# Four input homes for the feed-forwards, the variance of the weighted attention on VectorE, the causal mask in quarters

## Chip, cores and metric

One NeuronCore of a Trainium2 chip. The metric is device time in microseconds of one execution; a kernel's number is the median of its runs.

## The reference, cut to what matters

A batch of 64 sequences of 128 tokens and 128 features goes through four layers, each against a context of 77 tokens with 128 features. All tensors are float32.

```
x: [64, 128, 128]   context: [64, 77, 128]   16 heads
L0: att = softmax(causal(QK^T / sqrt(8))) V;  h = LayerNorm(att + x);  x = gelu(h W1 + b1) W2 + b2 + h
L1: att = softmax(mask(QK^T / sqrt(8) * weights)) V;  x = LayerNorm(x + att Wo + bo)      (LN_EPS 1e-5)
L2: att = softmax(mask(QK^T) / sqrt(128)) V;  h = LayerNorm(att Wo + bo + x);  x = LayerNorm(relu(h W1 + b1) W2 + b2 + h)
L3: n = RMSNorm(x);  x = x + segmented causal attention(n, 16 heads of 64, rotary) Wout;
    h = RMSNorm(x) W1 + b1;  a, g = split(h);  x = x + (silu(g) * a) W2 + b2
```

The causal mask of L0 forbids key k for query i when k > i: of 77 keys and 128 queries, queries 77 and later see all keys.

## The kernel before, in words

The layers are cut into seven stages that run one after another over all 64 batches: A0 and F0 (attention and feed-forward of L0), A1 (L1), A2 and F2 (L2), A3 and F3 (L3). Each stage reads its input from device memory and writes its output there. The program is written out by hand for each engine: for each stage an engine has a function `step(b, has)` that lists what it does in one step, for several batches at different depths of the pipeline, and `drive` runs the steps, the middle ones in a hardware loop of four. The engines meet only by counting semaphores, and every engine works its list in order. So the order in a step function is the order of execution, and a wait holds up all that stands behind it on that engine.

**Attention stages A0, A1, A2** (64 batches each). SyncE issues every DMA. TensorE (`cross_tensor`) computes, per batch, the keys, values and queries, the scores of 16 heads into four PSUM banks (four matmuls of 32 rows, one per group of four heads, line 668), transposes the probabilities in two halves of eight heads (line 686), and forms the attended values (line 703). In A0 the causal mask enters as a matmul of a bfloat16 identity with the tile `causal` (128 x 308: one 128 x 77 mask repeated for four heads), accumulated in PSUM before the scores: for banks 0 and 1 in `mask_early` at the end of the step before (line 650), for banks 2 and 3 at the head of `scores` (line 665). In A2 a bias per key is added behind the scores by four matmuls of one row (line 674). ScalarE takes the exponentials (line 769) and copies the transposed probabilities out of PSUM (line 774).

In A1 the scores are multiplied on VectorE by weights (line 886, two halves), masked by a `scalar_tensor_tensor` of the uint8 mask and the scores, both in SBUF (line 891, two halves), and reduced to a maximum (line 899); GpSimd subtracts the maximum (`shift`, line 1012, two halves: the second half of batch b first in its step, the first half of batch b + 1 later). The layer norm of batch b - 3 rides in the same steps: VectorE's `aggregate` (line 953) gives mean and variance; GpSimd adds the epsilon (line 1024), takes the power -1/2 (line 1026), and forms -mean x rstd (line 1035, a 128 x 1 result); ScalarE's `centre` computes z = t x rstd + that shift (line 820); GpSimd multiplies by gamma (line 1040) and adds beta (line 1043). GpSimd's step in A1, in order:

```
shift(b, 1); rstd(b - 3) [epsilon, power]; residual(b - 1); scale_mean(b - 3); shift(b + 1, 0); affine(b - 3) [gamma, beta]
```

and VectorE's: two `weigh`, `mask` of half 0, `invert`, `peak_masked` of half 0, `normalise`, `keep_v`, `sums`, `mask` of half 1, `statistics`, `peak_masked` of half 1, `aggregate`. In A0 and A2 GpSimd itself centres (line 1030).

**Feed-forward stages F0, F2, F3** (32 groups of two batches). TensorE (`ff_tensor`), per step: the hidden layer of group g (line 1154), the transposes of group g + 1 (line 1142), the down projection of group g - 1 (line 1168). The input of a group lies in `fx_s`, one tile per parity (two homes), loaded by `ff_sync` (line 1110) two groups ahead. A load waits until the home's last group has been transposed (in F3: normalised) and until GpSimd has added the bias to it (`residual`, line 1302). That residual of group g + 1 stands behind GpSimd's other work of the step; in F3 that is `rstd(g + 2)` (line 1312), which waits for VectorE's `squares(g + 2)` (line 1219), which waits for the load of group g + 2. VectorE in F3, per step: `norm(g + 1)` (line 1226), three `gate` (line 1234), `squares(g + 2)`, `total(g - 1)` (line 1247). The first two loads of a feed-forward stage are issued during the last steps of the stage before (`HEADS`, line 1935); the third waits in SyncE's list behind the last stores of that stage.

Of the kernel before, what the change touches and what calls it, by code (L numbers as in the profile page):

```python
# [138 lines left out]
def build_layers(nc, a, out):  # L139
# [3 lines left out]
    with ExitStack() as ctx:  # L143
# [31 lines left out]
        causal = sb("causal", [T, QC], BF16)  # L175
# [117 lines left out]
        shift_s = slots("mean_shift", [T, 1])  # L293
# [5 lines left out]
        fx_s = slots("fx", [T, GB, D])  # L299
# [44 lines left out]
        causal32, tri32 = wvo[:, 0:QC], wvo[:, 512:512 + HC * SEG]  # L344
        causal_loads = [(causal32, a["c_causal"])]
# [75 lines left out]
        mean_scaled = event("mean_scaled", ["A1"])  # L421
# [191 lines left out]
        def cross_tensor(pe, ph):  # L613
# [29 lines left out]
            def mask_early(b, values):  # L643
                if b.first:
                    pe.wait_ge(masks_made, 3)
                pe.wait_ge(k_kept.sem(b), k_kept.count(ph, b))
                if values:
                    pe.wait_ge(v_kept.sem(values), v_kept.count(ph, values))
                for c in range(2):
                    nc.tensor.matmul(bank[c][:, 0:QC], identb[:], causal[:], start=True, stop=False)  # L650

            def scores(b):
# [10 lines left out]
                if ph == "A0":  # L663
                    for c in range(2, NQ):
                        nc.tensor.matmul(bank[c][:, 0:QC], identb[:], causal[:], start=True, stop=False)
                for c in range(NQ):
                    rows = slice(32 * c, 32 * c + 32)
                    mm = nc.tensor.matmul(bank[c][:, 0:QC], qT_s[b.par][rows, :], kblk_s[b.par][rows, :],  # L668
                                          start=(ph != "A0"), stop=(ph != "A2"))
# [61 lines left out]
            def step(b, has):  # L731
# [28 lines left out]
                if has(2) and ph == "A0":  # L760
                    mask_early(b + 2, b + 1 if has(1) else None)
            drive(pe, NB, step, reach=REACH)

        def cross_scalar(act, ph):
# [52 lines left out]
            def centre(b):  # L817
                act.wait_ge(mean_scaled.sem(b), mean_scaled.count(ph, b))
                wait_earlier(act, zg_made, ph, b, 2)
                nc.scalar.activation(z_s[b.par][:], t_s[b.par][:], ACT.Identity, bias=shift_s[b.par][:, 0:1], scale=rstd_s[b.par][:, 0:1])\  # L820
                    .then_inc(z_made.sem(b), 1)

# [12 lines left out]
            def step(b, has):  # L835
# [17 lines left out]
                if has(-3) and weighted:  # L853
                    centre(b + -3)
# [8 lines left out]
        def cross_vector(dve, ph):  # L863
# [90 lines left out]

            def step_weighted(b, has):
                if has(1):
                    weigh(b + 1, 0)
                    weigh(b + 1, 1)
                    mask(b + 1, 0)
# [41 lines left out]
        def cross_gpsimd(pool, ph):  # L1001
# [20 lines left out]
            def rstd(b):  # L1022
                pool.wait_ge(mv_made.sem(b), mv_made.count(ph, b))
                nc.gpsimd.tensor_tensor(var_s[b.par][:], mv_s[b.par][:, 1:2], ln_eps[:, 0:1], ALU.add).then_inc(var_made.sem(b), 1)  # L1024
                pool.wait_ge(var_made.sem(b), var_made.count(ph, b))
# [6 lines left out]

            def scale_mean(b):

                nc.gpsimd.tensor_scalar(shift_s[b.par][:], mv_s[b.par][:, 0:1], rstd_s[b.par][:, 0:1], -1.0, ALU.mult, ALU.mult)\  # L1035
                    .then_inc(mean_scaled.sem(b), 1)
# [8 lines left out]
            def step(b, has):  # L1045
                weighted = ph == "A1"
                if weighted:
                    if has(0):
                        shift(b, 1)
                    if has(-3):  # L1050
                        rstd(b + -3)
                        wait_earlier(pool, z_made, ph, b + -3, 2)
                    if has(-1):
                        residual(b + -1)
                    if has(-3):
                        scale_mean(b + -3)
# [36 lines left out]
        def ff_sync(sp, ph):  # L1093
# [3 lines left out]
            def step(g, has):  # L1097
                if has(2):
                    n = g + 2

                    if (n + -2).exists:
                        sp.wait_ge(taken.sem(n + -2), taken.count(ph, n + -2))
                    if (n + -2).exists:
                        sp.wait_ge(fxb_made[ph].sem(n + -2), fxb_made[ph].count(ph, n + -2))
# [1038 lines left out]
```

## Time and profile before

| | |
|---|---|
| median of 3 runs | 2474.96 us (2472.53 to 2475.68) |
| the profiled execution, its time | 2471.87 us |
| its span, first to last instruction | 2470.1 us |
| mean granted TensorE clock | 0.985 of full |
| busy: TensorE, VectorE, ScalarE, GpSimd | 93%, 76%, 61%, 63% of the span |
| chain that ended last | TensorE 68%, GpSimd 16%, issue 6%, ScalarE 3%, VectorE 3%, DMA 2% |
| A0, F0 | about 0 to 383 us, 383 to 512 us |
| A1 (with the memory set-up before it), A2 | 512 to 961 us, 961 to 1312 us |
| F2, A3, F3 | 1312 to 1447 us, 1447 to 2320 us, 2320 to 2470 us |

"Busy" is the share of the span in which an engine has an instruction running. The chain is followed back from the last instruction: at each step to whatever released it. A line number names the line of the kernel that issued an instruction. In the views, PE is TensorE's matmul and PEld its weight load, DVE is VectorE, ACT ScalarE, POOL GpSimd, SPq SyncE's issue of a DMA. `sb_region` is one large tile in which the attention's working tiles are carved.

### The profile page before, as it was taken

How to read it: one execution, taken by the hardware profiler on the slowest of the kernel's cores; microseconds unless marked ns; L12 is line 12 of the kernel's file. 1: busy time of each engine (PE TensorE's matmuls, PEld its weight loads, DVE VectorE, ACT ScalarE, POOL GpSimd, SP SyncE). 2: the span in 40 equal slices, each digit the busy share in tenths (PEclk: the TensorE clock that was granted, in tenths of full speed). 3: DMA queues.
4: the chain of work that ended last, by engine and by line, in shares of the span. 5: the costliest groups of instructions: out<-in, count | busy, mean ns of one | idle time of the engine just before them, and what ended most of it. 6: DMA issues, size and time to landing. Idle time of an engine off the chain costs nothing.

```text
span 2470.1 us, 83369 instructions
## 1 busy us (share of the span) xinstructions
PE 2308.8 (93%) x26926; PEld 1812.7 (73%) x26926; DVE 1888.0 (76%) x4003; ACT 1498.6 (61%) x3408; POOL 1559.2 (63%) x2438
## 2 busy tenths in 40 slices
PE   7999998988888887999998989999999999999899
PEld 5777777976666665777777867777777777777687
DVE  5777772139999996777775678888888888888566
ACT  5777775549988996888885524444444444444433
POOL 2666663118999995666666766666666666666332
PEclk9999999979999998999999999999999999999999
DMA  4111111235555552222221223334333333333211
GB/s 128 43 43 42 42 42 55 72 96 164 162 162 159 165 162 49 52 50 51 50 50 52 67 76 95 93 96 97 96 94 95 94 94 95 93 94 93 54 58 53
DMA packets 443043, 211.78 MB, mean 86 GB/s; under 512 B 206400, under 2 KB 433856, under 8 KB 442816
## 3 DMA queue, kind: packets, MB, share of 16 engines
q1 hardware_dynamic: 442944, 210.51, 32.7%
q8 instruction: 56, 0.92, 0.2%
q14 instruction: 43, 0.35, 0.1%
HBM read 113.36 MB, written 29.88 MB: 58 GB/s over the span
## 4 chain that ended last, share of the span: by engine, by line
PE 68%; POOL 16%; issue 6%; ACT 3%; DVE 3%; DMA 2%; SPq 1%; POOLq 1%; DVEq 0%; ACTq 0%
PE bank L686 10%; PE bank L1463 9%; PE bank L1423 9%; POOL sb_region L1012 5%; PE bank L703 5%; PE bank L1491 5%; PE bank L1154 4%; PE bank L668 4%; PE bank L1168 4%; PE bank L1473 3%; PE bank L1449 3%; ACT sb_pT L774 3%; POOL sb_mean_shift L1035 2%; POOL sb_var L1024 2%; PE bank L1499 2%
## 5 line engine op out<-in xcount | busy, mean ns | idle before, releaser
L686 PE MATMUL bank<-sb_ident,sb_region 128*77 128x128 f32 x3072 | 413.1, 278 | 57.4 <-ACT sb_pT L774 54.0
L774 ACT ACTIVATE sb_pT<-bank 77x1024 f32<-77x1024 f32 x384 | 391.6, 1020 | 81.4 <-PE bank L686 80.4
L686 PEld LDWEIGHTS bank<-sb_ident,sb_region 128*77 128x77 f32 x3072 | 348.3, 151 | 112.1 <-issue 108.2
L1553 ACT ACTIVATE sb_l<-sb_l 128x640 f32<-128x640 f32 x128 | 94.5, 738 | 384.6 <-DVE sb_l L1601 384.6
L873 DVE TENSOR_REDUCE sb_max<-bank 128x8 f32<-128x616 f32 x256 | 203.1, 793 | 151.1 <-PE bank L668 80.3
L769 ACT ACTIVATE sb_region<-sb_region 128x616 f32<-128x616 f32 x384 | 276.9, 722 | 25.0 <-POOL sb_region L1012 24.9
L1680 POOL TENSOR_TENSOR sb_pn<-sb_l,sb_r_all 128x512 f32<-128x512 f32 x128 | 134.7, 1052 | 232.1 <-DVE sb_r_all L1611 224.2
L1423 PE MATMUL bank<-sb_region,sb_wqkv 128*128 128x128 f32 x2048 | 253.7, 278 | 5.8 <-DVE sb_region L1589 5.0
L1463 PE MATMUL bank<-sb_wvo,sb_region 128*64 128x512 f32 x1024 | 248.2, 606 | 0.0
L1423 PEld LDWEIGHTS bank<-sb_region,sb_wqkv 128*128 128x128 f32 x2048 | 241.9, 194 | 8.3 <-DVE sb_region L1589 5.6
L703 PEld LDWEIGHTS bank<-sb_pT,sb_v 77*32 77x32 f32 x6144 | 152.3, 110 | 93.4 <-issue 73.4
L703 PE MATMUL bank<-sb_pT,sb_v 77*32 77x128 f32 x6144 | 216.2, 277 | 3.8 <-ACT sb_pT L774 3.6
L878 DVE TENSOR_TENSOR sb_region<-bank,sb_max 128x616 f32<-128x616 f32 x256 | 204.6, 799 | 11.7
L1671 POOL TENSOR_TENSOR sb_region<-sb_region 128x512 f32<-128x512 f32 x128 | 162.6, 1270 | 72.6 <-PE bank L1449 64.5
L668 PE MATMUL bank<-sb_region,sb_qT 32*128 32x308 f32 x1536 | 158.2, 481 | 33.8 <-ACT sb_region L789 20.4
L1012 POOL TENSOR_TENSOR sb_region<-sb_region,sb_max 128x616 f32<-128x616 f32 x128 | 158.8, 1241 | 37.5 <-DVE sb_max L899 37.5
L1491 PEld LDWEIGHTS bank<-sb_region,sb_pT 128*64 128x64 f32 x2048 | 121.7, 137 | 77.4 <-issue 67.5
L1024 POOL TENSOR_TENSOR sb_var<-sb_mv,sb_ln_eps 128x1 f32<-128x1 f32 x192 | 68.0, 354 | 174.8 <-DVE sb_mv L953 174.8
L1203 ACT ACTIVATE sb_fh<-bank,sb_L_xattn_ffb 128x256 f32<-128x256 f32 x256 | 109.0, 472 | 113.7 <-PE bank L1154 113.7
L1537 ACT ACTIVATE sb_region<-bank 128x512 f32<-128x512 f32 x256 | 151.3, 593 | 41.5 <-PE bank L1463 32.0
L1589 DVE TENSOR_TENSOR sb_region<-bank,sb_sinT 128x512 f32<-128x512 f32 x256 | 174.0, 680 | 0.0
L1589 DVE TENSOR_TENSOR sb_region<-bank,sb_cosT 128x512 f32<-128x512 f32 x256 | 172.5, 674 | 1.6 <-PE bank L1423 1.5
(184 smaller groups left out, 5629.1 us busy)
## 6 DMA issues: line engine op xcount, KB each, us to landing
sb_region<-in_side SPq DMA_DIRECT2D x64, 616.0 KB, 3.8
sb_pT<-sb_region SPq DMA_DIRECT2D x512, 64.0 KB, 2.0
sb_kF<-sb_region SPq DMA_DIRECT2D x512, 64.0 KB, 2.2
scratch_after_A<-sb_y SPq DMA_DIRECT2D x256, 64.0 KB, 1.7
sb_fx<-scratch_after_A SPq DMA_DIRECT2D x96, 128.0 KB, 2.1
sb_mask<-in_mask SPq DMA_DIRECT2D x64, 154.0 KB, 2.3
sb_x<-scratch_after_F SPq DMA_DIRECT2D x128, 64.0 KB, 1.9
sb_ctx<-in_ctxT SPq DMA_DIRECT2D x192, 38.5 KB, 1.8
```

Source lines behind the costliest of these rows:

```text
L668: mm = nc.tensor.matmul(bank[c][:, 0:QC], qT_s[b.par][rows, :], kblk_s[b.par][rows, :], start=(ph != "A0"), stop=(ph != "A2"))
L686: mm = nc.tensor.transpose(two[0:C, h * T:(h + 1) * T], p_s[b.par][:, head * C:(head + 1) * C], ident[:])
L703: mm = nc.tensor.matmul(att_bank[32 * i:32 * i + 32, k * T:(k + 1) * T], v_s[b.par][:, first:first + 32], pT_s[k][:, h * T:(h + 1) * T], s ...
L769: nc.scalar.activation(half(p_s[b.par], k), half(p_s[b.par], k), ACT.Exp, scale=SCALE[ph]).then_inc(exp_made.sem(b), 1)
L774: nc.scalar.activation(pT_s[k][:], two[0:C, :], ACT.Copy).then_inc(pT_kept.sem(b), 1)
L873: nc.vector.tensor_reduce(dst, by_bank_and_head(scores_half(k)), AX.X, ALU.max).then_inc(max_made.sem(b), 1)
L878: nc.vector.tensor_tensor(by_bank_and_head(by_bank(half(p_s[b.par], k))), by_bank_and_head(scores_half(k)), spread_max(k), ALU.subtract).t ...
L1012: nc.gpsimd.tensor_tensor(by_head(half(p_s[b.par], k)), by_head(half(p_s[b.par], k)), spread(max_s[:, 8 * k:8 * k + 8], C), ALU.subtract)\
L1423: mm = nc.tensor.matmul(rope_bank[eo][:, n * T:(n + 1) * T], wqkv[:, col:col + 128], xnT_s[b.lap], start=True, stop=True)
L1463: mm = nc.tensor.matmul(vo_banks[g][r * SEG:(r + 1) * SEG, :], xnT_s[b.lap][:, g * SEG:(g + 1) * SEG], wvo[:, (2 * h + r) * HC * D:(2 * h ...
L1491: nc.tensor.matmul(out3_bank[g * SEG:(g + 1) * SEG, 0:D], pT_s3[h][:, c * T + g * SEG:c * T + (g + 1) * SEG], vo_s[h][:, (g * HC + c) * D: ...
L1589: ins = nc.vector.tensor_tensor(part[what][eo].rearrange("p (n t) -> p n t", t=T), src, table[:].unsqueeze(1).to_broadcast([128, BLOCKS, T ...
```

## The change

1. **A0's mask in quarters.** `mask_early` and the mask matmuls ahead of the scores go. The scores now open each bank's accumulation, and behind them come eight matmuls of 64 rows and 64 columns: per bank one for queries 0 to 63 and one for queries 64 to 127, from 64 x 64 pieces of the identity, placed so that four neighbouring ones use the four quarters of the array. The tile `causal` shrinks to 128 x 154 and is loaded by two DMAs in place of one; the wait for it becomes a wait for two.
2. **A1's layer norm.** GpSimd's addition of epsilon goes to VectorE (`variance`, between the second `weigh` and the first `mask`). GpSimd's `scale_mean` and ScalarE's `centre` go; GpSimd now centres itself, by the instruction that it uses in A0 and A2, at the place where `scale_mean` stood.
3. **Feed-forwards.** `fx_s` has four homes; a group is loaded four ahead, into the home of group n - 4, and waits besides for the load of group n - 2. The first four loads of a stage are issued in the last steps of the stage before.

```diff
-        causal = sb("causal", [T, QC], BF16)
+        causal = sb("causal", [T, 2 * C], BF16)
...
-        fx_s = slots("fx", [T, GB, D])
+        fx_s = slots("fx", [T, GB, D], n=LAPS)
...
-        causal32, tri32 = wvo[:, 0:QC], wvo[:, 512:512 + HC * SEG]
-        causal_loads = [(causal32, a["c_causal"])]
+        causal32, tri32 = wvo[:, 0:2 * C], wvo[:, 512:512 + HC * SEG]
+        causal_loads = []
+        for r in range(2):
+            both = a["c_causal"].rearrange("(g i) (h k) -> i g h k", g=2, k=C)
+            causal_loads.append((causal32[r * KH:(r + 1) * KH, :].rearrange("p (g k) -> p g k", k=C), both[:, :, 0, :]))
...
-            def mask_early(b, values):
-                if b.first:
+            def scores(b):
+                if ph == "A0" and b.first:
                     pe.wait_ge(masks_made, 3)
-                pe.wait_ge(k_kept.sem(b), k_kept.count(ph, b))
-                if values:
-                    pe.wait_ge(v_kept.sem(values), v_kept.count(ph, values))
-                for c in range(2):
-                    nc.tensor.matmul(bank[c][:, 0:QC], identb[:], causal[:], start=True, stop=False)
-
-            def scores(b):
...
-                if ph == "A0":
-                    for c in range(2, NQ):
-                        nc.tensor.matmul(bank[c][:, 0:QC], identb[:], causal[:], start=True, stop=False)
                 for c in range(NQ):
                     rows = slice(32 * c, 32 * c + 32)
                     mm = nc.tensor.matmul(bank[c][:, 0:QC], qT_s[b.par][rows, :], kblk_s[b.par][rows, :],
-                                          start=(ph != "A0"), stop=(ph != "A2"))
+                                          start=True, stop=(ph == "A1"), skip_group_check=(ph == "A0"))
+                if ph == "A0":
+                    for c in range(NQ):
+                        for g in range(2):
+                            r = (g + c) % 2
+                            rows = slice(r * KH, (r + 1) * KH)
+                            later = causal[rows, g * C:(g + 1) * C].unsqueeze(1).to_broadcast([KH, QH, C])
+                            mm = nc.tensor.matmul(bank[c][g * KH:(g + 1) * KH, 0:QC], identb[rows, r * KH:(r + 1) * KH], later,
+                                                  start=False, stop=True, skip_group_check=True)
...
-                if has(2) and ph == "A0":
-                    mask_early(b + 2, b + 1 if has(1) else None)
...
-            def centre(b):
-                act.wait_ge(mean_scaled.sem(b), mean_scaled.count(ph, b))
-                wait_earlier(act, zg_made, ph, b, 2)
-                nc.scalar.activation(z_s[b.par][:], t_s[b.par][:], ACT.Identity, bias=shift_s[b.par][:, 0:1], scale=rstd_s[b.par][:, 0:1])\
-                    .then_inc(z_made.sem(b), 1)
...
-                if has(-3) and weighted:
-                    centre(b + -3)
...
+            def variance(b):
+                dve.wait_ge(mv_made.sem(b), mv_made.count(ph, b))
+                nc.vector.tensor_scalar(var_s[b.par][:], mv_s[b.par][:, 1:2], LN_EPS, None, ALU.add).then_inc(var_made.sem(b), 1)
...
                 if has(1):
                     weigh(b + 1, 0)
                     weigh(b + 1, 1)
+                if has(-3):
+                    variance(b + -3)
+                if has(1):
                     mask(b + 1, 0)
...
                     if has(-3):
-                        rstd(b + -3)
-                        wait_earlier(pool, z_made, ph, b + -3, 2)
+                        root(b + -3)
                     if has(-1):
                         residual(b + -1)
                     if has(-3):
-                        scale_mean(b + -3)
+                        centre(b + -3)
...
-                if has(2):
-                    n = g + 2
+                if has(LAPS):
+                    n = g + LAPS
+
+                    if (n + -LAPS).exists:
+                        sp.wait_ge(taken.sem(n + -LAPS), taken.count(ph, n + -LAPS))
+                        sp.wait_ge(fxb_made[ph].sem(n + -LAPS), fxb_made[ph].count(ph, n + -LAPS))
 
                     if (n + -2).exists:
-                        sp.wait_ge(taken.sem(n + -2), taken.count(ph, n + -2))
-                    if (n + -2).exists:
-                        sp.wait_ge(fxb_made[ph].sem(n + -2), fxb_made[ph].count(ph, n + -2))
+                        sp.wait_ge(fx_loaded.sem(n + -2), fx_loaded.count(ph, n + -2))
...
-                    sp.dma_start(fx_s[n.par][:], pair_of(source[ph], n)).then_inc(fx_loaded.sem(n), 16)
+                    sp.dma_start(fx_s[n.lap][:], pair_of(source[ph], n)).then_inc(fx_loaded.sem(n), 16)
...
-            HEADS = {ph: () if ph == "A3" else (-2, -1) if ph in FFS else (-4, -3) for ph in order}
+            HEADS = {ph: () if ph == "A3" else (-4, -3, -2, -1) if ph in FFS else (-4, -3) for ph in order}
...
-            dve.wait_ge(causal_loaded, 1 * 16)
+            dve.wait_ge(causal_loaded, 2 * 16)
```

`LAPS` is 4. All readers of `fx_s` index it by `lap` instead of `par`. `root` is the second half of the old `rstd`: the wait for `var_made`, the power, and the wait for its own result.

## Rows read from the trace of the kernel before

**Rows 1.** Timeline, TensorE, one batch of A0: start, us, engine, line, out<-in, xcount, idle before.
```profile
201.29 1.07 PE L686 MATMUL bank<-sb_ident,sb_region 128*77 128x128 f32 x8 [0.25 <-ACT sb_pT L774]
...
202.81 0.80 PE L668 MATMUL bank<-sb_region,sb_qT 32*128 32x308 f32 x8
203.54 0.43 PE L703 MATMUL bank<-sb_pT,sb_v 77*32 77x128 f32 x8
```

**Rows 2.** Timeline, TensorE, the same steps in A2, which has no causal mask.
```profile
1024.42 1.07 PE L686 MATMUL bank<-sb_ident,sb_region 128*77 128x128 f32 x8
1025.48 0.80 PE L668 MATMUL bank<-sb_region,sb_qT 32*128 32x308 f32 x8
```

**Rows 3.** Timeline, TensorE, A3: four 64x64 tiles and what starts behind them.
```profile
1605.38 0.30 PE L1441 MATMUL bank<-sb_tri,sb_identb 64*64 64x256 bf16 x4
1605.52 0.73 PE L1449 MATMUL bank<-sb_kF,sb_pT 64*64 64x81 f32 x32
```

**Rows 4.** Window of A1: us, busy us (x instructions) of PE, PEld, DVE, ACT, POOL.
```profile
563.00:938.00 375.00, 314.47 (x4030) 241.62 (x4030) 354.52 (x715) 337.59 (x769) 348.42 (x476) 1.00 0.54 160
```

**Rows 5.** Timeline, VectorE and GpSimd, one batch of A1.
```profile
750.16 1.21 POOL L1012 TENSOR_TENSOR sb_region<-sb_region,sb_max 128x616 f32<-128x616 f32 x1
...
750.92 1.12 DVE L891 SCALAR_TENSOR_TENSOR sb_region<-sb_mask,sb_region 128x616 f32<-128x616 uint8 x1
...
751.34 0.75 POOL L1024 TENSOR_TENSOR sb_var<-sb_mv,sb_ln_eps 128x1 f32<-128x1 f32 x1
...
752.16 0.55 POOL L1026 TENSOR_TENSOR sb_rstd<-sb_var,sb_minus_half 128x1 f32<-128x1 f32 x1
...
753.37 1.01 POOL L1035 TENSOR_SCALAR sb_mean_shift<-sb_mv,sb_rstd 128x1 f32<-128x1 f32 x1
753.46 0.79 DVE L891 SCALAR_TENSOR_TENSOR sb_region<-sb_mask,sb_region 128x616 f32<-128x616 uint8 x1
```

**Rows 6.** Timeline, A1 near its start: a root issued just after a mask.
```profile
561.92 0.79 DVE L891 SCALAR_TENSOR_TENSOR sb_region<-sb_mask,sb_region 128x616 f32<-128x616 uint8 x1
...
562.04 1.08 POOL L1026 TENSOR_TENSOR sb_rstd<-sb_var,sb_minus_half 128x1 f32<-128x1 f32 x1
```

**Rows 7.** Groups by line: the centring as GpSimd does it in A0 and A2.
```profile
L1030 POOL TENSOR_SCALAR sb_z<-sb_t,sb_mv,sb_rstd 128x128 f32<-128x128 f32 x128 | 102.1, 797 | 0.4
```

**Rows 8.** One line: VectorE's tensor_scalar in F2, ns min/median/max.
```profile
L1273 DVE TENSOR_SCALAR sb_fc<-sb_ft,sb_fmv x64: 286/519/795, 1325.0 to 1445.0; 128x128 f32<-128x128 f32 x64
```

**Rows 9.** Timeline, head of F0: residual, third load, TensorE.
```profile
390.28 1.40 POOL L1302 TENSOR_TENSOR sb_fxb<-sb_fx,sb_L_xattn_ffb 128x256 f32<-128x256 f32 x2
391.07 1.07 SPq L1110 DMA_DIRECT2D sb_fx<-scratch_after_A  x2
...
393.31 0.62 PE L1142 MATMUL bank<-sb_ident,sb_fx 128*128 128x128 f32 x2 [4.26 <-DMA sb_fx<-scratch_after_A]
...
396.97 1.89 PE L1154 MATMUL bank<-sb_fxT,sb_L_xattn_ffw 128*128 128x256 f32 x8
```

**Rows 10.** Waits of TensorE in F2, from 1318 to 1440 us: total, times, longest.
```profile
PE bank L1142 <- DMA sb_fx<-scratch_after_A: 1.8, 2, 1.4
```

**Rows 11.** Timeline, TensorE in F3: four starts of down projections.
```profile
2327.89 1.50 PE L1168 MATMUL bank<-sb_w2g,sb_fh 128*128 128x128 f32 x12
...
2450.74 1.50 PE L1168 MATMUL bank<-sb_w2g,sb_fh 128*128 128x128 f32 x12
...
2454.89 1.50 PE L1168 MATMUL bank<-sb_w2g,sb_fh 128*128 128x128 f32 x12
...
2463.38 2.84 PE L1168 MATMUL bank<-sb_w2g,sb_fh 128*128 128x128 f32 x24
```

**Rows 12.** Timeline, F3: from one load of the input to the next residual.
```profile
2375.84 0.38 SPq L1110 DMA_DIRECT2D sb_fx<-scratch_after_A  x1
...
2378.27 0.29 DVE L1219 CUSTOM_DVE_ANT_0 sb_fsq<-sb_fx 128x128 f32<-128x128 f32 x1 [0.75 <-DMA sb_fx<-scratch_after_A]
...
2379.62 0.72 POOL L1302 TENSOR_TENSOR sb_fxb<-sb_fx,sb_L_xattn_ff_b 128x256 f32<-128x256 f32 x1
```

More of the change, by code:

```diff
@@ L292, in build_layers @@
         rstd_s = slots("rstd", [T, 1])
-        shift_s = slots("mean_shift", [T, 1])
         z_s = slots("z", [T, D])
@@ L420, in build_layers @@
         rstd_made = event("rstd_made", CROSS)
-        mean_scaled = event("mean_scaled", ["A1"])
         z_made = event("z_made", CROSS)
@@ L1024, in rstd, with root @@
                 nc.gpsimd.tensor_tensor(var_s[b.par][:], mv_s[b.par][:, 1:2], ln_eps[:, 0:1], ALU.add).then_inc(var_made.sem(b), 1)
+                root(b)
+            def root(b):
                 pool.wait_ge(var_made.sem(b), var_made.count(ph, b))
@@ L1031, in centre @@
                                         ALU.subtract, ALU.mult).then_inc(z_made.sem(b), 1)
-            def scale_mean(b):
-                nc.gpsimd.tensor_scalar(shift_s[b.par][:], mv_s[b.par][:, 0:1], rstd_s[b.par][:, 0:1], -1.0, ALU.mult, ALU.mult)\
-                    .then_inc(mean_scaled.sem(b), 1)
             def affine(b):
@@ L1140, in transpose_x @@
                         pe.wait_ge(fx_loaded.sem(g), fx_loaded.count(ph, g))
-                        src = fx_s[g.par][:, k, :]
+                        src = fx_s[g.lap][:, k, :]
                     mm = nc.tensor.transpose(fx_bank[g.par][:, k * T:(k + 1) * T], src, ident[:])
@@ L1218, in squares @@
                 for k in range(GB):
-                    nc.vector.tensor_tensor_reduce(fsq_s[k][:], fx_s[g.par][:, k, :], fx_s[g.par][:, k, :], 1.0 / D, RMS_EPS, ALU.mult, ALU.add,
+                    nc.vector.tensor_tensor_reduce(fsq_s[k][:], fx_s[g.lap][:, k, :], fx_s[g.lap][:, k, :], 1.0 / D, RMS_EPS, ALU.mult, ALU.add,
                                                    fvar_s[g.par][:, k:k + 1]).then_inc(fstats_made.sem(g), 1)
@@ L1225, in norm @@
                     dve.wait_ge(fxT_made[ph].sem(g + -2), fxT_made[ph].count(ph, g + -2))
-                nc.vector.tensor_tensor(fz_s[g.par][:], fx_s[g.par][:], spread(frstd_s[g.par][:], D), ALU.mult).then_inc(fz_made[ph].sem(g), 1)
+                nc.vector.tensor_tensor(fz_s[g.par][:], fx_s[g.lap][:], spread(frstd_s[g.par][:], D), ALU.mult).then_inc(fz_made[ph].sem(g), 1)
             def gate(g):
@@ L1301, in residual @@
                     pool.wait_ge(ft_made.sem(g + -2), ft_made.count(ph, g + -2))
-                nc.gpsimd.tensor_tensor(fxb_s[g.par][:], fx_s[g.par][:], every(b2), ALU.add).then_inc(fxb_made[ph].sem(g), 1)
+                nc.gpsimd.tensor_tensor(fxb_s[g.par][:], fx_s[g.lap][:], every(b2), ALU.add).then_inc(fxb_made[ph].sem(g), 1)
             def rstd(g):
```

## Prediction

> **What bounds the kernel now.** I read the page first: TensorE is busy for 93% of the span and makes up 68% of the chain that ended last, GpSimd 16%. Such shares are an average over seven stages, so I cut the trace into windows by stage, followed the chain of waits in one steady batch of each stage that the change touches, and read the timeline where stages meet.
>
> In A0 the chain of a batch runs through TensorE and one ScalarE copy. From the transposes of half 1 to the scores it is 1.52 us (202.81 - 201.29), from the scores to the attended values 0.73 us, 2.25 us together [rows 1]; the mask matmuls lie inside, nothing covers them.
>
> In A1 a batch takes 6.3 us (375 us hold 476 GpSimd instructions, eight a batch) with VectorE busy 95%, GpSimd 93%, ScalarE 90% [rows 4]. GpSimd never rests, but part of its busy time is waiting: the mask of VectorE and GpSimd's instructions shut each other out. The mask was issued at 750.92 and ended at 752.04, 0.67 us after GpSimd's shift ended at 751.37; the epsilon sum, one element a row, took 0.75 us, until that mask was done; the shift of the mean, also one element, took 1.01 us, until the next mask ended at 754.25 [rows 5].
>
> F0 and F2 are bound by TensorE except at their heads, where the third load is late. F3 is bound by a loop: a load is issued at 2375.84, the squares start at 2378.27, the residual ends at 2380.34, and only that lets the next load go, 4.5 us later and more [rows 12]. TensorE needs 4.15 us a group where nothing holds it (2450.74 to 2454.89) and gets one in 4.52 us on average (2327.89 to 2463.38, thirty intervals) [rows 11].
>
> **F3.** The load four ahead is freed by the same residual, but is needed two groups later, so the 2.4 us from issue to squares leave the loop. The squares then follow the gates, the root is done while TensorE runs its down projection, and the next bound is TensorE at 4.15 us. Full gain 30 x 0.37 = 11 us. VectorE's normalisation may still collide with GpSimd's residual and hold a gate, so I take **10 us**, range 6 to 11.5. The added wait for load n - 2 is met two groups before; behind it on SyncE stand the output stores, which nobody waits for until the group after next.
>
> **Head of F0.** Today the third load is issued at 391.07, after the residual of group 0 has started behind the tail of A0; TensorE idles 4.26 us until 393.31 and reaches the next hidden layer at 396.97 [rows 9]. With four loads in place it goes on at 389.05 with two transposes and a down projection: twelve such matmuls show 1.50 us [rows 11], sixteen and the transposes about 2.15 us, so the hidden layer starts at 391.2. Gain 5.8 us; I take **6**, range 5 to 6.5. It holds more than the idle time because the matmuls behind the gap ran slowly (3.66 us from 393.31 to 396.97 for the same work). **Head of F2:** the same wait is 1.8 us [rows 10]; **1.5 us**. The first four loads cost SyncE two more issues during A0, A2 and A3, about half a microsecond each [rows 9], where SyncE has slack.
>
> **A0.** The four mask matmuls leave the stretch before the scores. What remains there is what A2 shows: 1.06 us from the transposes to the scores (1025.48 - 1024.42) [rows 2], not 1.52 less four masks, because matmuls of another tile shape don't follow on at once. Behind the scores come two rounds of four quarters. In A3 four tiles of 64 x 64 with 256 columns let the next matmul start 0.14 us later [rows 3]; with 308 columns 0.17, two rounds 0.34 us. The quarters add one more change of tile shape; the one from the transposes to the scores costs about 0.2 us (1.06 us for eight transposes, which stream in some 0.86 if each takes an eighth of 1.07 less the last one's tail), and I take half of it for this one, between nothing and 0.2. New path 1.06 + 0.73 + 0.34 + 0.1 = 2.23, without that 0.1 and with perfect overlap of 0.26 it is 2.05. I take 2.19, a gain of 0.06 on 62 batches: **4 us**. Bounds: 0.20 gained a batch (12 us); two quarters at a time and not four, 0.16 lost (10 us). The page TensorEngine Tiling of the Trainium skill, section Tiling Modes, says that changing the tile shape drains the engine. The trace agrees, by the 0.2 us just named; by the rule the quarters cost a drain that masks of full height did not, and without it A0 would gain 0.10 more a batch. The wait for keys, formerly in part ahead of the early masks, is met: GpSimd's `block_keys` ends before the transposes do.
>
> **A1.** Count from the end M of mask 0, 752.04. Today the root starts at M + 0.12 and ends at M + 0.67, the mean's shift is released by mask 1 at about M + 2.3, and the second shift follows [rows 5]. Changed: the variance is on VectorE before mask 0, which anyway waits 0.45 us (750.92 to 751.37), so the root's input is ready when the shift ends, and the root is itself shut out by mask 0. How that ends the trace shows: a root issued 0.12 us after a mask ended 0.41 us behind it (563.12 against 562.71) [rows 6]. So root until M + 0.42; gap and residual take 0.66 today (752.71 to 753.37), less a little for a wait that goes: M + 1.0. Then the centring, 0.80 us [rows 7], until M + 1.8. Mask 1 is issued at M + 1.42 and finds the centring running: it ends 0.67 us after its release, M + 2.47. The second shift begins there and not at M + 2.3. Of the 0.17 lost I give back 0.1, as an instruction that is shut out has its start behind it (the root needed 0.41 after release, 0.55 when free [rows 5, 6]). The variance itself: nothing if it ends inside the wait of mask 0; if it is shut out too, at most 0.17, the 0.29 us of the fastest `tensor_scalar` [rows 8] less the 0.12 that the mask saves when shut out (0.67 for 0.79) [rows 5]. I take 0.05. Sum +0.12 us on 60 batches, **7 us lost**. ScalarE is relieved of a copy that was not on its path to the scores. Bounds: 0.25 gained (the root's 0.25 comes through) and 0.6 lost (rival 3). The page SBUF - State Buffer, section Who interferes with whom, says that `tensor_scalar` with both ends in SBUF can use two ports and then shuts GpSimd out, or is shut out, for a whole instruction. It speaks against both moved pieces. The same operation of VectorE in F2 takes 286 ns at best and 519 at the median [rows 8], so the trace agrees for 128 x 128; for one element a row nothing here shows it. By the rule A1 would lose 14 us and not 7.
>
> **Start.** One more DMA issue ahead of the first loads: **0.5 us** lost [rows 9].
>
> **Sum:** -10 - 6 - 1.5 - 4 + 7 + 0.5 = -14 us. Against the profiled execution, 2471.87, that is 2458; its time is 3.1 us below the median of 2474.96, against which the result is measured: **2461 us**.
>
> **Rivals.** (1) A1 gains: GpSimd holds the ports for only part of the centring, so mask 1 isn't delayed, and the earlier root counts, 0.2 gained a batch, 12 us. Sum -14 - 7 - 12 = -33: 2442, and 2434 with A0 at its good bound. For it: the centring computes long on few elements; against it: the mask waited for the full shift. Chance 0.2. (2) Only the feed-forwards pay: the quarters run two at a time, A0 loses 10 us. Sum 0, 2475. For it: nothing in A0 shows quarters; against it: A3 does. Chance 0.07. (3) Slower. In A1 GpSimd's work and VectorE's masks never overlap: root 0.42, gap and residual 0.66, centring 0.8, mask 0.79, shifts 2.42, gamma and beta about 0.9 (what today's 6.3 leaves), variance 0.17 and mask 0.71 add to 6.9 us against 6.3 now: +0.6 on 60 batches, 36 us lost and not 7. Sum +15: 2490. The place is mask 1 against the centring; it decides from +0.35 a batch, where the other gains (21 us) are eaten. For it: both engines are at 93% and above; against it: an instruction that is shut out keeps its start. Chance 0.08. (4) The change does not free F3: the normalisation collides every time and a group still takes 4.5 us. Sum -4, 2471. Chance 0.08. (5) The variance is shut out each time, and mask 0 with it, 0.12 + 0.12 a batch: A1 loses 14 us, sum -7: 2468. Chance 0.12. The forecast, between 2450 and 2466: 0.45.
>
> **How the numbers follow.** The measurement tells about 0.2%, 5 us, from no change. Faster by more: the forecast, rival 1, most of 5 and a part of 4, **0.77**. Within: rival 2, the rest, **0.14**. Slower: rival 3 and the far end of 2, **0.09**. The range of eight in ten takes the forecast, most of rival 1 and of 4 and 5: **2441 to 2475**.
>
> **What would show it.** F3: no wait of the squares for a DMA, starts of the down projections 4.15 to 4.25 us apart. F0: no idle time of 4 us near 389. A0: transposes to scores 1.06 us, scores to attended values 1.1 to 1.2 us. A1: mask 1 at 1.0 to 1.3 us instead of 0.79, mask 0 unchanged, the root at 1.1 us, a batch at 6.4 us. It is wrong if A1's batch is under 6.2 or over 6.6 us, or if scores to attended values in A0 is above 1.3 us.

## The result and the profile after

The new kernel took 2441.57 us (median of 4 runs, 2439.34 to 2442.62) against 2475.32 for the kernel before: 0.9865 of it, 95% interval 0.9847 to 0.9882. That is 33.8 us less, where 14 were forecast. It lies at the very edge of the range (2441 to 2475), and on rival 1 (2442).

The profiled executions differ by 29.3 us (2442.62 less 2471.87; spans 2440.8 and 2470.1). To see where these went I took the time line of TensorE and compared the start of the same matmul at the end of each stage. Differences to the kernel before in us, stretch by stage:

| stretch, to | forecast | new | homes alone | A1 alone | quarters alone |
|---|---|---|---|---|---|
| last scores of A0 | -3.5 | -4.0 | -1.8 | +0.7 | -3.9 |
| last hidden layer of F0 | -6 | -4.5 | -3.9 | 0.0 | +1.3 |
| last scores of A1 | +7 | **-8.8** | +1.8 | **-9.0** | -1.9 |
| last scores of A2 | 0 | -1.6 | -0.1 | -0.3 | +0.7 |
| last hidden layer of F2 | -1.5 | -5.2 | -6.1 | -1.5 | -0.2 |
| first masks of A3 | 0 | +2.5 | +3.4 | -0.1 | +0.9 |
| last masks of A3 | 0 | +0.7 | +3.5 | +4.6 | 0.0 |
| last hidden layer of F3 | -10 | -8.5 | -10.1 | +0.5 | +0.1 |

(The last three columns are told below.) Stretches that an edit does not touch differ by up to 2 us, A3 by up to 4.6, and one profiled execution may lie some us from its kernel's median; a single entry means no more than that. The entry that matters is A1's: it has the wrong sign.

The chain that ended last, by engine, in the new kernel's page: GpSimd's share fell from 16% to 12%.

```profile
PE 70%; POOL 12%; issue 8%; ACT 4%; DVE 2%; SPq 1%; DMA 1%; POOLq 0%; DVEq 0%; ACTq 0%
```

**A1**, window of the new kernel that answers to [rows 4] (us, then busy us and instructions of PE, PEld, DVE, ACT, POOL): GpSimd is as busy as before, with seven instructions a batch in place of eight, and VectorE has got idle time (355 to 341 us).

```profile
563.00:938.00 375.00, 311.65 (x4055) 247.00 (x4053) 340.89 (x776) 315.12 (x707) 351.79 (x430) 0.99 0.53 157
```

Time line of VectorE and GpSimd in one batch, which answers to [rows 5]:

```profile
737.72 1.22 POOL L1008 TENSOR_TENSOR sb_region<-sb_region,sb_max 128x616 f32<-128x616 f32 x1
...
738.63 0.14 DVE L946 TENSOR_SCALAR sb_var<-sb_mv 128x1 f32<-128x1 f32 x1
...
738.69 0.90 DVE L880 SCALAR_TENSOR_TENSOR sb_region<-sb_mask,sb_region 128x616 f32<-128x616 uint8 x1
...
738.89 1.12 POOL L1025 TENSOR_TENSOR sb_rstd<-sb_var,sb_minus_half 128x1 f32<-128x1 f32 x1
...
740.67 0.80 POOL L1029 TENSOR_SCALAR sb_z<-sb_t,sb_mv,sb_rstd 128x128 f32<-128x128 f32 x1
...
741.02 0.79 DVE L880 SCALAR_TENSOR_TENSOR sb_region<-sb_mask,sb_region 128x616 f32<-128x616 uint8 x1
...
741.44 1.44 POOL L1008 TENSOR_TENSOR sb_region<-sb_region,sb_max 128x616 f32<-128x616 f32 x1
```

Mask 0 ends at M = 739.59 (738.69 + 0.90). The root ends at 740.01, M + 0.42, as forecast; the centring begins at 740.67, M + 1.1, and ends at M + 1.9, each 0.1 us later than forecast. Mask 1 is issued at 741.02, M + 1.43, as forecast, with the centring running. The forecast let it wait until the centring had ended. It did not wait: it took 0.79 us, and the centring beside it 0.80. What is shut out is the shift behind them, which ends at 742.88, M + 3.3. Before, it ended at M + 3.5 (754.34 + 1.21 less 752.04), in the time line of [rows 5]:

```profile
754.34 1.21 POOL L1012 TENSOR_TENSOR sb_region<-sb_region,sb_max 128x616 f32<-128x616 f32 x1
```

The next mask 0 then finds less of the shift of half 1 in its way: between 590 and 900 us it takes 1.00 us on average, where it took 1.22 before. The forecast had it unchanged. That is 0.22 us a batch, less the 0.06 by which the added sum delays it; a batch takes 6.16 us in place of 6.32 (mean distance of the scores, 600 to 880 us).

One line each, over the whole run: the centring (min/median/max in ns), and the added sum on VectorE.

```profile
L1029 POOL TENSOR_SCALAR sb_z<-sb_t,sb_mv,sb_rstd x192: 792/797/906, 38.3 to 1297.2; 128x128 f32<-128x128 f32 x192
L946 DVE TENSOR_SCALAR sb_var<-sb_mv x64: 142/144/155, 554.5 to 932.6; 128x1 f32<-128x1 f32 x64
```

The first shows that the centring is not disturbed even once in A1: at most 906 ns in 192, and that also as the most in A0 and A2 before (907). The second takes 0.14 us at the median. In this batch mask 0 starts 0.02 us before the second `weigh` ends; in the batch of [rows 5] it started 0.08 us before. So the sum delays it by 0.06.

**A0**, time line of TensorE in one batch, which answers to [rows 1]:

```profile
199.98 1.07 PE L685 MATMUL bank<-sb_ident,sb_region 128*77 128x128 f32 x8 [0.25 <-ACT sb_pT L771]
...
201.04 0.80 PE L659 MATMUL bank<-sb_region,sb_qT 32*128 32x308 f32 x8
...
201.77 0.47 PE L667 MATMUL bank<-sb_causal,sb_identb 64*64 64x308 bf16 x8
...
202.17 1.08 PE L702 MATMUL bank<-sb_pT,sb_v 77*32 77x128 f32 x32
```

Transposes to scores 1.06 us, scores to quarters 0.73, quarters to attended values 0.40: 2.19 in all, each as forecast (0.34 + 0.1 for the quarters).

**Head of F0**, time line of TensorE, answering to [rows 9], and the granted clock (last columns: PEclk, DMA share, GB/s) in two windows of it:

```profile
380.32 3.49 PE L1149 MATMUL bank<-sb_fxT,sb_L_xattn_ffw 128*128 128x256 f32 x8 [0.53 <-ACT sb_fxT L1184]
...
384.65 1.99 PE L1149 MATMUL bank<-sb_fxT,sb_L_xattn_ffw 128*128 128x256 f32 x8 [0.62 <-ACT sb_fxT L1184]
...
388.49 1.89 PE L1149 MATMUL bank<-sb_fxT,sb_L_xattn_ffw 128*128 128x256 f32 x8
```

```profile
381.00:382.00 1.00, 1.00 (x4) 0.82 (x3) 0.93 (x6) 0.99 (x2) 0.82 (x2) 0.50 0.00 0
384.00:386.00 2.00, 1.38 (x7) 1.22 (x7) 0.00 (x0) 1.21 (x4) 1.73 (x4) 1.00 0.14 41
```

The first two hidden layers in the kernel before:

```profile
383.90 1.99 PE L1154 MATMUL bank<-sb_fxT,sb_L_xattn_ffw 128*128 128x256 f32 x8 [0.53 <-ACT sb_fxT L1189]
...
387.05 2.00 PE L1154 MATMUL bank<-sb_fxT,sb_L_xattn_ffw 128*128 128x256 f32 x8 [0.94 <-ACT sb_fxT L1189]
```

The wait of 4.26 us is gone. But the first hidden layer now takes 3.5 us where it took 2.0: the granted clock is at its lower level (0.50, 1.2 GHz) at 381 us, as the first hidden layer starts. Before, it fell at 393, behind the wait. From the second hidden layer to the third it is now 3.84 us (384.65 to 388.49) where it was 9.92 (387.05 to 396.97), 6.1 less; from the first to the second it is 4.33 where it was 3.15, 1.2 more.

**F3**, time line, answering to [rows 11, 12]: down projections, the addition of the bias on GpSimd and the normalisation on VectorE in two groups.

```profile
2383.64 1.50 PE L1163 MATMUL bank<-sb_w2g,sb_fh 128*128 128x128 f32 x12
...
2385.78 0.73 POOL L1297 TENSOR_TENSOR sb_fxb<-sb_fx,sb_L_xattn_ff_b 128x256 f32<-128x256 f32 x1 [0.24 <-DVE sb_ft L1242]
...
2385.89 0.90 DVE L1221 TENSOR_TENSOR sb_fz<-sb_fx,sb_frstd 128x256 f32<-128x256 f32 x1 [0.19 <-issue]
...
2388.00 1.50 PE L1163 MATMUL bank<-sb_w2g,sb_fh 128*128 128x128 f32 x12
...
2390.04 0.43 DVE L1221 TENSOR_TENSOR sb_fz<-sb_fx,sb_frstd 128x256 f32<-128x256 f32 x1
...
2390.14 0.91 POOL L1297 TENSOR_TENSOR sb_fxb<-sb_fx,sb_L_xattn_ff_b 128x256 f32<-128x256 f32 x1 [0.23 <-DVE sb_ft L1242]
...
2392.15 1.50 PE L1163 MATMUL bank<-sb_w2g,sb_fh 128*128 128x128 f32 x12
```

The squares no longer wait for a load. For most of the stage the groups take 4.15 and 4.36 us by turns. In the long ones the addition (2385.78) starts ahead of the normalisation (2385.89), which then takes 0.90 us in place of 0.43 and holds up a gate; in the short ones the normalisation is first and it is the addition that takes 0.91, which costs nothing: that group takes 4.15 us.

### The profile page after: what moved, and what is told of

It reads as the page before. It is cut to its first block, busy times and chain, and to the rows that moved or that the text cites. A ratio compares the mean times of both kernels' runs of the same rounds, so it can differ in the third digit from the quotient of the medians.

```text
span 2440.8 us, 83677 instructions
## 1 busy us (share of the span) xinstructions
PE 2287.5 (94%) x27182; PEld 1807.3 (74%) x27182; DVE 1872.0 (77%) x4067; ACT 1474.2 (60%) x3344; POOL 1562.2 (64%) x2374
## 4 chain that ended last, share of the span: by engine, by line
PE 70%; POOL 12%; issue 8%; ACT 4%; DVE 2%; SPq 1%; DMA 1%; POOLq 0%; DVEq 0%; ACTq 0%
PE bank L685 10%; PE bank L1458 9%; PE bank L1418 9%; PE bank L1149 6%; PE bank L702 5%; PE bank L1486 5%; PE bank L659 4%; PE bank L1163 4%; POOL sb_region L1008 4%; ACT sb_pT L771 3%; PE bank L1468 3%; PE bank L1444 3%; POOL sb_rstd L1025 2%; PE bank L1494 2%; POOL sb_z L1029 2%
## 5 line engine op out<-in xcount | busy, mean ns | idle before, releaser
L702 PE MATMUL bank<-sb_pT,sb_v 77*32 77x128 f32 x6144 | 208.8, 276 | 3.2 <-ACT sb_pT L771 3.2
L1666 POOL TENSOR_TENSOR sb_region<-sb_region 128x512 f32<-128x512 f32 x128 | 162.6, 1270 | 72.4 <-PE bank L1444 61.9
L1008 POOL TENSOR_TENSOR sb_region<-sb_region,sb_max 128x616 f32<-128x616 f32 x128 | 173.2, 1353 | 38.4 <-DVE sb_max L888 38.4
L1667 POOL TENSOR_TENSOR sb_region<-sb_region 128x512 f32<-128x512 f32 x128 | 165.9, 1296 | 0.0
```

Source lines behind the costliest of these rows:

```text
L702: mm = nc.tensor.matmul(att_bank[32 * i:32 * i + 32, k * T:(k + 1) * T], v_s[b.par][:, first:first + 32], pT_s[k][:, h * T:(h + 1) * T], s ...
L1008: nc.gpsimd.tensor_tensor(by_head(half(p_s[b.par], k)), by_head(half(p_s[b.par], k)), spread(max_s[:, 8 * k:8 * k + 8], C), ALU.subtract)\
```

## The experiments

**Each part alone.** Three kernels, each the kernel before with one part of the change: the homes; A1's layer norm; the quarters.

```diff
# homes
-        fx_s = slots("fx", [T, GB, D])
+        fx_s = slots("fx", [T, GB, D], n=LAPS)
...
# A1
-                        rstd(b + -3)
+                        root(b + -3)
...
-                        scale_mean(b + -3)
+                        centre(b + -3)
...
# quarters
-                    mask_early(b + 2, b + 1 if has(1) else None)
```

> The kernel before with the feed-forwards' part alone: four homes, loads four groups ahead. If the parts add up as the two traces put them: 8 us come from F3 (groups alternate between 4.15 and 4.36 us instead of 4.52 on average), 4 from F0, 3 from F2 with its hand-over to A3, together 15 us less, and A0 and A1 keep their batches of 5.56 and 6.3 us. If instead part of what the new kernel gains in the feed-forwards comes from the other two parts (an earlier end of A0 or A2), it is under 10 us.

> The kernel before with the part in A1 alone: variance on VectorE, centring on GpSimd, no sum and no shift of the mean there, no copy on ScalarE. Theory (the centring and the mask of VectorE run side by side): a batch takes 6.15 us, 9 us less in all. Forecast on record (the mask waits for the centring): 7 us more. If the gain in A1 is owed to the part in A0 or to the loads, no change.

> The kernel before with the quarter masks alone. As forecast: from the transposes to the scores 1.06 us, from the scores to the attended values 1.13, a batch of A0 5.50 us instead of 5.565, 4 us less in A0, and 0.5 us given back at the start: 3.5 us less. If the A0 gain of the new kernel is owed to something else, A0 keeps 5.565 us.

Measured: homes 2455.35 us, 0.9918 of the kernel before (0.9906 to 0.9931); A1 2464.26, 0.9961 (0.9949 to 0.9973); quarters 2470.51, 0.9988 (0.9980 to 0.9997). With 2473.54 before, that is 18, 9 and 3 us less, 30 together for the 34 of the whole: the parts add up within their intervals. The batches are as expected: in A0 5.50 us (median distance of the scores) with the quarters and 5.57 without, in A1 6.16 with A1's part and 6.33 without. The homes gave 3 us more than expected; with them alone only every fourth group of F3 is a long one, and F3 gains 10.1 us. So the gain of A1 belongs to A1's part.

**Which half of A1's part?** The centring on GpSimd, with the epsilon sum left there. Against the kernel with A1's part alone:

```diff
                if has(-3):
-                    variance(b + -3)
...
-                        root(b + -3)
+                        rstd(b + -3)
```

> The kernel before with the centring of A1 on GpSimd, the epsilon sum left there too. Theory (the centring runs beside the mask; the second shift starts when mask 1 ends, M + 2.2, whether the variance is early or late): sum until M + 0.12, root until M + 0.67, add until M + 1.33, centring M + 1.33 to 2.13, mask 1 M + 1.43 to 2.22, second shift until M + 3.3 as in the new kernel: 6.15 us a batch, 9 us less. Rival (the gain comes from the variance on VectorE): no change within 2 us, or slower, since GpSimd does 0.8 us of work that ScalarE did.

Measured: 2508.01 us, 1.0141 (1.0126 to 1.0157), 34 us **more**. Neither; the rival's "or slower" gave no such size, and its reason, the extra work, is in the new kernel too. Time line of a batch of the more frequent kind:

```profile
741.56 1.53 POOL L1027 TENSOR_SCALAR sb_z<-sb_t,sb_mv,sb_rstd 128x128 f32<-128x128 f32 x1
...
741.63 0.79 DVE L881 SCALAR_TENSOR_TENSOR sb_region<-sb_mask,sb_region 128x616 f32<-128x616 uint8 x1
```

Here the mask is issued 0.07 us behind the centring's start, and the centring takes 1.53 us: it ends 0.67 us after the mask does. The mask is not delayed. Between 590 and 900 us 29 of 44 batches look like this; in 13 others the centring meets no mask and takes 0.80 us. What differs here from the new kernel is the sum itself, 0.75 us on GpSimd, and with it the lead. That gave the next theory: what counts is by how much GpSimd's instruction starts ahead of the mask. The other half alone, the sum on VectorE with the shift of the mean and ScalarE's centring kept:

```diff
+                if has(-3):
+                    variance(b + -3)
...
                     if has(-3):
-                        rstd(b + -3)
+                        root(b + -3)
```

> The kernel before with only the variance moved: the epsilon sum of A1 on VectorE, the shift of the mean on GpSimd and the centring on ScalarE as before. Theory (what counts is the lead of GpSimd's instruction over mask 1: one whose start is 0.35 us ahead runs undisturbed, one 0.07 ahead is shut out): root until M + 0.42, add until M + 1.08, the shift of the mean issued 0.35 us ahead of mask 1 is over in 0.26 us, at M + 1.34. The second shift then starts ahead of mask 1 (M + 1.43) and the mask waits until it ends at M + 2.55: mask 1 takes 1.8 us instead of 0.79 and the batch grows by 0.3 to 0.8 us, 20 to 50 us more in all. Rival (the whole gain of A1 is the sum that left GpSimd): 9 us less.

Measured: 2467.77 us, 0.9980 (0.9970 to 0.9989), 4 us less, and 5.6 us less in the stretch of A1. The sign was missed. The shift of the mean behaved as foretold (0.27 us, undisturbed), but in 36 of 49 batches the mask then went ahead of the second shift, of 616 elements, though that had started before it:

```profile
751.27 0.27 POOL L1045 TENSOR_SCALAR sb_mean_shift<-sb_mv,sb_rstd 128x1 f32<-128x1 f32 x1
...
751.49 2.00 POOL L1019 TENSOR_TENSOR sb_region<-sb_region,sb_max 128x616 f32<-128x616 f32 x1
...
751.63 0.79 DVE L891 SCALAR_TENSOR_TENSOR sb_region<-sb_mask,sb_region 128x616 f32<-128x616 uint8 x1
```

Only in 13 batches did the mask wait for the shift, 1.58 us.

**The lead, changed by itself.** The new kernel, mask 1 one instruction earlier:

```diff
-                if has(-2):
-                    sums(b + -2)
                 if has(1):
                     mask(b + 1, 1)
                 if has(-2):
+                    sums(b + -2)
                     statistics(b + -2)
```

> The new kernel with mask 1 of A1 ahead of the sum with the residual on VectorE, so that the mask is issued 0.15 us behind the centring's start and not 0.35. Theory A (the centring needs the shared access for well under 0.15 us): centring and mask both keep 0.8 us, the second shift is shut out 0.2 us less, a batch takes 5.95 us instead of 6.15: 12 us less than the new kernel. Theory B (it needs it for 0.15 to 0.35 us): the centring is shut out and takes about 1.4 us, a batch 6.5: 20 us more than the new kernel.

Measured: 2471.03 us, 0.9994 (0.9984 to 1.0004): 29 us above the new kernel's 2441.57 (33 by the distance of each to the kernel before beside it), and the stretch of A1 is 28 us longer than there. A batch of A1 takes 6.67 us, 0.51 more, and nearly all of that stands at mask 0, which takes 1.48 us on average in place of 1.00, as the shifts behind the centring come later. This is theory B, dearer than its 20 us.

```profile
741.65 1.60 POOL L1028 TENSOR_SCALAR sb_z<-sb_t,sb_mv,sb_rstd 128x128 f32<-128x128 f32 x1
...
741.80 0.79 DVE L880 SCALAR_TENSOR_TENSOR sb_region<-sb_mask,sb_region 128x616 f32<-128x616 uint8 x1
```

All batches of A1 between 590 and 900 us in these kernels, by the time from the start of GpSimd's instruction to that of mask 1 (us, read off the time lines):

| kernel | GpSimd's instruction | lead | it took | mask 1 took |
|---|---|---|---|---|
| centring alone | centring | 0.06 to 0.08 (29 batches) | 1.52 to 1.54 | 0.79 |
| mask earlier | centring | 0.14 to 0.15 (35) | 1.59 to 1.61 | 0.79 |
| mask earlier | centring | 0.29 to 0.30 (11) | 1.58 to 1.59 | 0.79 |
| centring alone | centring | 0.33 to 0.34 (2) | 0.80 | 0.79 |
| centring alone | centring | no mask beside it (13) | 0.80 | - |
| new, A1 alone | centring | 0.34 to 0.50 (50 each) | 0.80 | 0.79 |
| before | shift of the mean | -0.01 to 0.25 (49) | 0.91 to 1.08 | 0.79 |
| variance alone | shift of the mean | 0.26 to 0.57 (49) | 0.27 | 0.79; 1.5 to 1.6 from 0.51 on |

The edge for the centring lies between 0.30 and 0.33 us. Below it the centring ends 0.5 to 0.7 us after the mask; above it the two run side by side, for 0.3 us or more. The one-element instruction takes 0.27 us undisturbed. With a lead of 0.25 or less it ends 0.05 to 0.13 us after the mask; with 0.26 or more it is over as the mask starts. So its rows don't show two instructions side by side; they show that it can be held by a mask that starts 0.25 us after it. In no batch did the centring delay the mask.

**The lead given back.** The kernel with the centring alone, with VectorE's statistics moved ahead of mask 1:

```diff
+                if has(-2):
+                    statistics(b + -2)
                 if has(1):
                     mask(b + 1, 1)
-                if has(-2):
-                    statistics(b + -2)
```

> The kernel with the centring on GpSimd and the epsilon sum left there, but the batch-norm statistics of VectorE ahead of mask 1 instead of behind it, so that the mask is issued 0.6 us behind the centring's start and not 0.07. Theory (a lead of 0.33 us or more leaves both undisturbed): the centring takes 0.80 us in place of 1.53, mask 1 keeps 0.79, and 10 to 25 us of the 34 that this kernel lost come back, though the mask itself is 0.5 us later. Rival (the loss is owed to the sum on GpSimd and mask 0 behind it, not to the lead): the centring may be short, but the time stays within 5 us of the kernel with the centring alone, or grows.

Measured: 2500.97 us, 1.0123 (1.0106 to 1.0140), 29 us above the kernel before beside it: 5 us of the 34 came back (4 in the stretch of A1), less than the theory said and within the rival's bound; the two intervals overlap.

```profile
741.91 0.80 POOL L1027 TENSOR_SCALAR sb_z<-sb_t,sb_mv,sb_rstd 128x128 f32<-128x128 f32 x1
...
742.68 1.21 POOL L1006 TENSOR_TENSOR sb_region<-sb_region,sb_max 128x616 f32<-128x616 f32 x1
...
742.78 1.76 DVE L881 SCALAR_TENSOR_TENSOR sb_region<-sb_mask,sb_region 128x616 f32<-128x616 uint8 x1
```

The centring takes 0.80 us in every batch, so the lead does what the theory says of it. But the lead became 0.87, not 0.6, and the mask, now 0.10 us behind the start of the second shift, waits for it: 1.76 us. There is an upper end to the useful lead as well: the mask has to come in before the shift. Nor is the rival's reason shown: mask 0 takes 0.79 us in every batch here, and 1.25 on average with the centring alone, against 1.22 before. So one loss took the place of another, and no run prices the short lead of the centring-alone kernel by itself; the earlier mask does that for the new kernel.

**A0: the place or the quarters?** The kernel before with its four masks of full height behind the scores:

```diff
+                if ph == "A0":
+                    for c in range(NQ):
+                        mm = nc.tensor.matmul(bank[c][:, 0:QC], identb[:], causal[:], start=False, stop=True)
```

> The kernel before with the four masks of full height behind the scores of A0. Theory (the place gives 0.46 us, 1.52 less 1.06; the masks cost 0.13 us each behind the scores, with no change of tile behind them): from the scores to the attended values 1.25 us, a batch 2.31 us on the path instead of 2.25, A0 4 us longer than before; the quarters then are worth 0.12 us a batch, 8 us. Rival (the place alone gives the gain): a batch of 5.50 us as with the quarters, 4 us less than before.

Measured: 2484.27 us, 1.0050 (1.0034 to 1.0066), 12 us more. Theory right in sign, low in size:

```profile
200.91 0.80 PE L658 MATMUL bank<-sb_region,sb_qT 32*128 32x308 f32 x8
...
201.65 0.70 PE L662 MATMUL bank<-sb_causal,sb_identb 128*128 128x308 bf16 x4
...
202.28 1.08 PE L696 MATMUL bank<-sb_pT,sb_v 77*32 77x128 f32 x32
```

Four masks take 0.63 us before the attended values start, not 0.52; a batch takes 5.75 us. The quarters do it in 0.40, so they are worth 0.23 us a batch, 14 us, and without them the new place would lose.

**F3: the collision.** The new kernel, the addition of F3 behind the normalisation, tried twice, the second time beside the new kernel again:

```diff
                if has(1):
+                    if has(2) and ph == "F3":
+                        pool.wait_ge(fz_made[ph].sem(g + 2), fz_made[ph].count(ph, g + 2))
                    residual(g + 1)
```

> The new kernel with GpSimd's addition of the bias in F3 behind the normalisation of VectorE, not beside it. Theory (every second group loses 0.2 us because the two shut each other out): all groups take 4.15 us, 3 us less than the new kernel. Rival (the 4.36 us come from TensorE or the gates): no change.

> The new kernel again, beside the next one on the same chip: 0.9865 of the kernel before.

> The new kernel with the addition of F3 behind the normalisation, a second time. Theory (3 us less in F3): 0.9853 of the kernel before, 3 us less than the new kernel beside it; rival: the same as the new kernel.

```profile
2380.60 0.42 DVE L1221 TENSOR_TENSOR sb_fz<-sb_fx,sb_frstd 128x256 f32<-128x256 f32 x1
...
2381.17 0.73 POOL L1297 TENSOR_TENSOR sb_fxb<-sb_fx,sb_L_xattn_ff_b 128x256 f32<-128x256 f32 x1 [0.73 <-DVE sb_fz L1221]
...
2382.78 1.50 PE L1163 MATMUL bank<-sb_w2g,sb_fh 128*128 128x128 f32 x12
...
2386.93 1.50 PE L1163 MATMUL bank<-sb_w2g,sb_fh 128*128 128x128 f32 x12
...
2391.08 1.50 PE L1163 MATMUL bank<-sb_w2g,sb_fh 128*128 128x128 f32 x12
```

Every group takes 4.15 us. From the first to the last hidden layer F3 is 11.4 us shorter than before in both profiles, against 8.5 and 7.1 in the new kernel's two: the 3 us of the theory or a little more. The whole: 2440.58 us (0.9866, 0.9843 to 0.9889) the first time, the same ratio as the new kernel's 0.9865; the second time 2436.63 (0.9857, 0.9840 to 0.9874) beside 2439.39 of the new kernel (0.9869, 0.9852 to 0.9885), 2.8 us lower with intervals that overlap. So the gain is shown in the stage, not in the whole.

## Why the prediction was wrong

- **A1, the failed step**: "Mask 1 is issued at M + 1.42 and finds the centring running: it ends 0.67 us after its release, M + 2.47." It ended at M + 2.2, undisturbed in each batch. The price 0.67 came from a mask behind a shift of 616 elements, which held the mask nearly to its end; it was applied to an instruction of 128 elements that held it in no batch. The gain then comes through at mask 0, 1.00 us in place of 1.22, which the forecast had unchanged; so the term of A1, +7, measured -8.8, and a batch of 6.16 us met the forecast's own sign of being wrong (under 6.2). I had written that mechanism down as rival 1, with nearly the right result for A1 (12 us gained, 9 measured), and gave it 0.2. The steps around it held: root at M + 0.42, centring at M + 1.1, mask issued at M + 1.43. My own sum thus had the centring 0.42 us ahead of the mask, and the 49 instructions of the kernel before, of one element and with leads of 0.25 at most, could not speak about that.
- **The Trainium skill**, page SBUF - State Buffer, section Who interferes with whom, calls the pair of ports that VectorE shares with GpSimd an exclusive lock, says of an instruction of VectorE with two SBUF inputs that it contends with GpSimd's reads, and that issue order decides who blocks. For the centring the runs disagree: issued first, it ran for 0.45 us of its 0.80 beside a mask of two SBUF inputs, and neither was longer; and with a lead of 0.30 us or less it was issued first and yet was the one held. Nor was the sum of one element on VectorE ever shut out (0.15 us at most, beside a shift of GpSimd), so rival 5, whose rule stands on the same page, did not happen.
- **Rival 3** (36 us lost in A1, mask 1 against the centring) had the place right: with the lead gone, the earlier mask lost 29 us and the centring alone 34, of which the lead given back returned 5, against a new wait of mask 1. In the new kernel the sum has left GpSimd and the lead is 0.34 us or more. The two halves are worth -4 and +34 alone and -9 together.
- **F3**: 8.5 for 10, the rest being the collision that the step named; the cause is shown by the kernel that removes it. Rival 4 did not happen.
- **Head of F0**: 4.5 for 6. The wait went as forecast; the slow clock that the step counted as part of the gain did not go, it came earlier. In one of the profiles with four homes (the second of the later addition) it stayed at full level there, and F0 gained 5.7; in the others with four homes 3.9 to 4.7. What decides where the clock falls in the thin tail of A0 was not tried.
- **F2**: 2.7 us (5.2 less 2.5 given back before the first masks of A3) for 1.5. Missed: beyond the head of F2 the loads were just late as well. The waits of the kernel before from 1350 to 1436 us (total, times, longest) have this line, which I did not see as I had asked for TensorE's matmuls and not for its weight loads:

```profile
PEld bank L1142 <- DMA sb_fx<-scratch_after_A: 4.5, 11, 0.7
```

- **A0 and the start**: 4.0 for 3.5; all parts of the step within 0.04 us. Rival 2 is out. The page TensorEngine Tiling (Array Packing) of the Trainium skill, section Tiling Modes, was weighed there (a change of tile shape drains the array): the 0.1 us taken for it fits the 0.06 that 0.40 leaves over two rounds of 0.17, and no run separates it further.
- **The sum**: -14 forecast. Replacing A1's +7 by its -8.8 alone gives -30, against -29.3 in the profiled pair and -33.8 in the medians: the other errors nearly cancel. That rival 1's total of 2442 is met so closely is in part luck: it had A1 3 us too good, and the profiled pair shows 4 us less than the medians.

## What to carry to other kernels

When VectorE and GpSimd shut each other out, the length of an instruction need not be what it blocks: a centring of 0.80 us that led by 0.34 us blocked nothing. Read the pairs off the trace by the lead of one start over the other, and check that the lead of the changed order is one that the trace has seen; if it isn't, the case is open and deserves an even chance. Then look where the time comes through: here it was not at the mask beside the centring but at the next one. Two edits that are each harmless or harmful alone can have the opposite sign together, since one sets the lead on which the other depends. And ask for the waits of TensorE's weight loads along with those of its matmuls.

## What the runs showed that was not expected

- GpSimd's centring of 128 elements (0.80 us) shares with a mask of two SBUF inputs once its start is 0.33 us or more ahead; at 0.30 us or less it is held until the mask ends (1.6 us). The mask is not delayed in either case.
- A shift of 616 elements behaves otherwise, and not by lead alone: a mask issued 0.04 to 0.15 us behind its start went first when the shift followed the one-element instruction (variance alone), and waited at 0.10 us when it followed the centring (lead given back), and at 0.03 us where the mask was mask 0 (centring alone). Why is open; that the recorded starts of GpSimd stand ahead of its first access by different amounts would fit, and was not tested.
- Masks of full height behind the scores cost 0.16 us each (0.63 for four), quarters 0.05 (0.40 for eight).
